# Second sort of a routed decoder layer: tiles 3 and 4 ranked one turn earlier, tile 3 scattered ahead of the next root

## The reference, cut to what matters

```
x = layernorm(x + attn(x))
# second part: expert e = min(clip(id) // 3125, 3); gate, up and down matrices are all ctx[e]
y = (silu(x @ ctx[e].T) * (x @ ctx[e].T)) @ ctx[e].T          # one expert of 256 x 256 per token
x = layernorm(x + y)
# third part: router of 4 experts, the largest is taken, weighted by its probability
probs = softmax(x @ Wr + br);  e = argmax(probs)
y = ((silu(x @ Wg[e]) * (x @ Wu[e])) @ Wd[e]) * probs[e]       # 256 -> 1024 -> 256
x = layernorm(x + y)
```

## Time and profile before

| what | us |
|---|---|
| median of 3 runs | 183.04 |
| the runs | 182.78, 183.04, 183.89 |
| the profiled execution | 183.68 |
| its span, first to last instruction | 182.0 |
| TensorE busy, VectorE busy | 169.0, 123.1 |

### The profile page before, as it was taken

One profiled execution on the slowest core, in us unless ns is written; L12 is line 12 of the kernel. 1 busy time (PEld: TensorE's weight loads), 2 busy tenths in 40 slices (PEclk: granted clock), 3 DMA queues, 4 the chain that ended last, 5 costly groups with the idle time before them and its releaser, 6 DMA issues.

```text
span 182.0 us, 3735 instructions
## 1 busy us (share of the span) xinstructions
PE 169.0 (93%) x947; PEld 125.8 (69%) x947; DVE 123.1 (68%) x393; ACT 95.0 (52%) x246; POOL 104.7 (58%) x125
## 2 busy tenths in 40 slices
PE   7999998899998999999999999999999999999910
PEld 2687776457876643878877788867888587867710
DVE  3388788869686777755655374444699966877780
ACT  3257979625466614347783466635666322545540
POOL 8100666552918574225997999953688700365563
PEclk9999999999999999999999999999999999999995
DMA  4999999257899723156937675274860004411101
GB/s 141 373 312 422 382 389 356 77 150 199 327 342 370 289 100 95 53 132 248 315 95 266 192 326 177 81 260 183 297 217 7 4 0 150 199 58 58 50 27 44
DMA packets 14405, 35.30 MB, mean 194 GB/s; under 512 B 1838, under 2 KB 8112, under 8 KB 14258
## 3 DMA queue, kind: packets, MB, share of 16 engines
q1 hardware_dynamic: 12752, 31.84, 50.3%
q0 software_dynamic: 1344, 3.22, 4.9%
q10 hardware_dynamic: 290, 0.01, 0.1%
HBM read 26.44 MB, written 8.88 MB: 194 GB/s over the span
## 4 chain that ended last, share of the span: by engine, by line
PE 72%; issue 8%; POOL 8%; DVE 5%; DMA 3%; ACT 1%; POOLq 1%; DVEq 0%
PE bank L588 12%; PE bank L589 11%; PE bank L590 11%; PE bank L596 6%; PE bank L786 4%; POOL out_tokens L577 4%; PE bank L901 4%; PE bank L878 3%; POOL rstd L500 3%; PE bank L749 3%; PE bank L659 3%; PE bank L690 3%; PE bank L602 2%; DMA x_sorted<-buf,slot 2%; PE bank L891 2%
## 5 line engine op out<-in xcount | busy, mean ns | idle before, releaser
L496 POOL TENSOR_TENSOR w_lo<-stage,w_hi 128x512 fp32r<-128x512 f32 x40 | 50.9, 1298 | 22.1 <-ACT w_hi L984 17.0
L1100 ACT ACTIVATE gate<-bank 128x256 f32<-128x256 f32 x40 | 15.4, 385 | 42.0 <-PE bank L590 36.4
L1477 DVE TENSOR_TENSOR hid<-bank,gate 128x256 f32<-128x256 f32 x40 | 17.0, 425 | 29.4 <-ACT gate L1100 29.1
L588 PE MATMUL bank<-w_hi,xr 128*128 x72 | 29.6, 411 | 0.5 <-DVE xr L1411 0.3
L500 POOL TENSOR_TENSOR rstd<-mv,mhalf 128x1 f32<-128x1 f32 x16 | 9.7, 604 | 34.1 <-DVE mv L1247 34.1
L589 PE MATMUL bank<-w_lo,xr 128*128 x72 | 28.4, 394 | 0.0
L590 PE MATMUL bank<-w_hi,xr 128*128 x72 | 28.2, 392 | 0.0
L984 ACT ACTIVATE w_hi<-stage 128x512 fp32r<-128x512 f32 x45 | 26.9, 631 | 1.4 <-PE bank L590 0.9
L588 PE MATMUL bank<-w_hi,hT 128*128 x72 | 23.4, 324 | 0.1
L589 PE MATMUL bank<-w_lo,hT 128*128 x72 | 20.3, 282 | 0.0
L590 PE MATMUL bank<-w_hi,hT 128*128 x72 | 20.3, 282 | 0.0
(11 more groups left out here) (228 smaller groups left out, 342.4 us busy)
## 6 DMA issues: line engine op xcount, KB each, us to landing
stage<-in_w_ffn SPq DMA_DIRECT2D x15, 768.0 KB, 6.0
arena<-in_w_ffn SPq DMA_DIRECT2D x8, 768.0 KB, 5.0
rows<-x_sorted SPq DMA_DIRECT2D x19, 132.0 KB, 2.3
x_sorted<-xr SPq DMA_DIRECT2D x2, 1056.0 KB, 7.1
x_sorted<-xr SPq DMA_DIRECT2D x1, 1584.0 KB, 14.3
buf<-in_x_tok SPq DMA_DIRECT2D x1, 1024.0 KB, 11.6
w_hi<-in_ctx SPq DMA_DIRECT2D x1, 1024.0 KB, 11.8
w_hi<-in_ctxT SPq DMA_DIRECT2D x1, 1024.0 KB, 14.3
```

Source lines behind the costliest of these rows:

```text
L496: g.tensor_tensor(out=lo, in0=src, in1=hi.bitcast(F32), op=ALU.subtract).then_inc(split_lo, 1)
L588: mm(dst, xhi, whi, start=start, stop=False)
L1100: a(gate[:, (T + j) % 2, :], fA[j % 2][:, 0:FQ], ACT.Silu).then_inc(silu_done, 1)
L1477: v.tensor_tensor(out=hid[:, (T + j) % 2, :], in0=fA[j % 2][:, FQ:2 * FQ], in1=gate[:, (T + j) % 2, :], op=ALU.mult).then_inc(h_done, 1)
```

## The change

Four moves of instructions; nothing is added or removed.

```diff
             scatter2(1)
             scatter2(2)
-            root2(2)
             pool.wait_ge(d_init2[1], 16)
             scatter2(3)
+            root2(2)
             scatter2(4)
...
                 if 1 <= i <= T:
                     th(i - 1)
-                if i == 9:
+                if i == 8:
                     rank(1)
...
                 if i == 7:
                     variances(1)
-                    residual(5)
+                    residual_sum(5)
                     shifts(1)
                     choose(1)
+                    residual_moments(5)
                 if i == 8:
+                    place(1)
                     residual(6)
                     variances(2)
-                    place(1)
```

## The result

The changed kernel takes 183.63 us (median of 20 runs, 182.49 to 185.12) against 182.88 us of the kernel before (median of 20, 182.21 to 183.89): a ratio of 1.0041, with a 95% interval of 1.0023 to 1.0060. So it is slower by 0.75 us, which lies within 1% of no change and is clear of its own interval. The forecast was +0.5 us, at 183.5.

What follows compares the result with a forecast made beforehand. TensorE's stream with its idle products and the scatters with the row load were taken to bound the kernel, meeting at 70.6. `rank(1)`'s wait, +0.45, made stage 4 about +0.50 late: 183.04 + 0.50 = 183.5 us, range 182.8 to 184.4.

Steps and rivals of the forecast that it cites:

- TensorE's stream and the scatters end together at 70.6, so nothing could be won: Start of stage 4: idle products end at 70.58, rows arrive for 70.62; earlier scatters alone win at most about 0.25 us.
- The exchange on VectorE costs nothing: VectorE, tile 5's moments behind `choose(1)`: mask 0.79 earlier, `hidden(8)` within 0.12 of its place, no cost.
- `rank(1)` waits for the mask, and this is the cost: TensorE behind `th(7)`: `rank(1)` waits for the mask ending at 58.25, so `down(6)` starts at 58.57, +0.45.
- TensorE's own stall is not there: Rival, chance 0.12: without the 0.87 stall ahead of `th(6)`, `rank(1)` holds TensorE from 57.25 to 58.25, +1.0, time 184.0.
- Behind the first transposes the delay stays as it is, and stage 4 is unchanged: From `ftx(0)` on, TensorE's chain passes the +0.50 on to the end, with no event keeping its own time.
- The signs of being wrong: `rank(1)` without a wait; `root2(2)` ahead of 61; `ftx(0)` at or ahead of 70.6; granted clock below 1.00 between 58 and 65.
- A waiting scatter starts 0.86 behind its slot: GpSimd's scatters: start at the later of 0.30 behind the one before and 0.86 behind `slot`; tile 3's at 60.41.
- The estimate by the Trainium skill: Shorter scatter start: tile 3's at 59.7, ending 60.7; `root2(2)` only +0.2, loss only `rank(1)`'s 0.45.
- `root2(2)` is delayed by 0.80 but hidden: GpSimd behind tile 3's scatter: `root2(2)` at 61.47 instead of 60.67; at most 0.10 shows on TensorE at `down(9)`.
- The price forecast for the root alone: Follow-up run's forecast: kernel before with only `root2(2)` behind `scatter2(3)`, holding `down(9)`: about +1.8 us, ratio 1.010.
- The scatter of tile 6 follows `rank(2)`: End of the scatters: group 2's `slot` waits for `rank(2)`, +0.45, so tile 6's scatter starts at 66.27 instead of 65.82.
- The clock does not fall: Against a rival, chance 0.03: the wait at `rank(1)` lowers TensorE's clock; 190.1 if all work until the idle products slows.

Runs made afterwards that it cites:

- experiments 2 and 6: Changed kernel, `rank(1)` behind `down(6)`: 1.0001; plus `root2(2)` before `scatter2(3)`: 0.9981; plus tile 8's offset load ahead of stage 2: 1.0004. Kernel before, that load moved, `place(1)` behind `hidden(9)`: 0.9995.
- the changed kernel with the offset early: Changed kernel with TensorE's load of tile 8's context offset moved from the end of `up(7)` to ahead of stage 2: 184.00 us, ratio 1.0041 against the kernel before.

## Why the prediction was right, point by point

**TensorE's stream and the scatters end together at 70.6, so nothing could be won.** Right. Eight fewer idle products left the start of stage 4 where it was (16.94 against 16.89 behind `th(6)`), and of the experiments that keep the offset's load in its place none starts stage 4 less than 16.86 behind `th(6)`. What binds is the scatter of tile 6, with 6.39 to 6.53 us behind it in all fourteen profiles.

**The exchange on VectorE costs nothing.** Right: 9.21 against 9.20 us on TensorE, ratio 1.0017 with 1 in its interval.

**`rank(1)` waits for the mask, and this is the cost.** Right in the mechanism, shown from both sides by the times: with the moves on TensorE and VectorE alone the whole loss is there (1.0047), with `rank(1)` one block later it is gone (1.0001). The term was forecast as 0.45 and comes out as 12.05 - 11.67 = 0.38 for the stall of the profile before (2.47 to `th(6)`). What it depends on was not foreseen. `root2(1)` starts 3.13 to 3.14 us behind `rank(0)` in all fourteen profiles (56.07 - 52.94 before, rows 5; 55.65 - 52.52 after), and the mask hangs on it and doesn't follow TensorE. So with a shorter stall the wait at `rank(1)` is longer, 0.54, 0.86 and 1.29 us in three profiles, while the kernel before gains what the stall loses. The rival "TensorE's own stall is not there", which got 0.12, describes this mechanism.

**Behind the first transposes the delay stays as it is, and stage 4 is unchanged.** This step failed. Stage 4 starts 0.32 later in the profile after, where 0.50 was forecast, and then loses 0.70 more ahead of L878, where nothing was: ScalarE waits there for a load of weights, and L878 hangs on it through VectorE. The two make 1.02, the medians 0.75.

**So the number came out right in part by luck.** Two accounts of the 0.75 are open. Two profiles of the kernel before and the four with the change's order on TensorE and VectorE give about 0.35 to the start of stage 4 and 0.6 inside it, 0.9 together. The other account is that most executions of the kernel before have a shorter stall than its profiles. With the mean of ten profiles, 2.11, it would start stage 4 at 16.89 + 2.11 = 19.00, 0.70 ahead of the changed one. But its only two profiles both show 2.47, and with the 0.58 lost inside stage 4 on the average the sum would be 1.28, beyond the interval of the measurement (0.42 to 1.10). Neither is shown, and single profiles and medians differ by up to 0.9 elsewhere too (experiments 2 and 6).

**The signs of being wrong.** Two came true as they were written: `root2(2)` stands at 60.68, ahead of 61, and `ftx(0)` at 70.52, ahead of 70.6. They were given in times from the span's start, and `rank(0)` came 0.42 earlier in this execution. Counted from it, `root2(2)` is 0.43 and `ftx(0)` 0.32 later than before (18.00 against 17.68), so the mechanism stands, but the signs could not have told.

**A waiting scatter starts 0.86 behind its slot.** Right: 0.84 in the profile after, and 0.84 again in the changed kernel with the offset early, where the slot ends at 59.25 and the scatter starts at 60.09. (In the run with GpSimd's list alone changed it starts 0.84 behind the slot too, at 61.07, but the page names `norm2` as what came last.) The estimate by the Trainium skill, "DMA: Bandwidth & Descriptors", section "Anatomy of one DMA" (dispatch and semaphore update together some 0.15), is not what the rows show here.

**`root2(2)` is delayed by 0.80 but hidden.** Half right. Its delay against `rank(0)` is 8.16 - 7.73 = 0.43, since `place(1)` comes earlier with a short stall too, and it is hidden as long as TensorE is late itself. Where TensorE is not, it shows: with `rank(1)` behind `down(6)` the loads wait 0.83 for the mask at `rank(2)`. The price forecast for the root alone, 1.8 us, was measured as 1.7. I had looked for its effect at `down(9)`; it comes first at `rank(2)`, ahead of it.

**The scatter of tile 6 follows `rank(2)`.** Right: 65.77 - 52.52 = 13.25 behind `rank(0)`, against 65.82 - 52.94 = 12.88: +0.37, where 0.45 was forecast.

**The clock does not fall.** Right for the change: in the profile after the granted clock reads 1.00 in every stretch from 40 to 72 us. That reading alone is weak, since it is 1.00 also from 1 to 5 us in the profile before, where ten products took 4.45 us (rows 7). But the loads of the twenty idle products take 4.00 us before and after. With fewer idle products the mean clock does fall in some executions.

## What to carry to other kernels

An instruction that is moved ahead on the engine that bounds must not outrun its producer: find what the producer hangs on, and count both from a mark ahead of the change, not from the span's start. A new wait whose end keeps its own time costs the difference to that time, not a fixed amount, so it grows when a stall ahead of it shrinks. One block further back, the same early work cost nothing by the times. And follow a delay to the end of the kernel: in the profiles here more of the loss arose some 35 us behind the change, after a wait for a load, than at the change itself.

## What was not expected of the hardware

**A register load can stall TensorE's queue for over a microsecond.** The load of tile 8's offset took 0.98 to 1.69 us in ten profiles, and mostly 0.30 at other places of the same loop. The two loads ahead of it took 0.95 to 1.01 in the profiles before and after, hidden behind running products. The core's DMA share was 1.00 at the time (the stretches of 50 to 60 us), and 0.64 from 40 to 45 us, where the loads took about 0.30. But the load of tile 9, at 56.3 and with the same share, took 0.30 too in eight of the ten profiles, and 0.63 and 0.70 in the other two. So load on the DMA engines alone doesn't explain it, and the cause stays open. Moved to 37.8 us, in the changed kernel, the load took 0.38.

**Work that nobody reads can be worth its time.** Eight idle products fewer move no start by more than 0.05 us, yet cost about 0.4% (1.0039, interval 1.0009 to 1.0070), through executions whose mean clock is 0.975 instead of 0.98 to 0.99.

**One load's length moves the whole end.** ScalarE's wait for the weights ahead of L984 was 0.38 us in the profile before and 1.35 after, and L878 came 0.70 later in stage 4. The load had been issued 5.5 us before that wait ended in the one and 6.4 in the other. No experiment tests why.
